# Layer one's sums over windows of 512 sorted edge rows in place of 1024, with three of each eight one-hots made on ScalarE

## The chip, the core and the metric

The kernel runs on one core of a Trainium2 chip. The core has five engines that run their own instruction streams and meet at semaphores: TensorE (PE in the profile, with its weight loads as PEld), VectorE (DVE), ScalarE (ACT), GpSimd (POOL) and SyncE (SP, here only an issuer of DMAs). The metric is the device time of one execution in microseconds, lower is better.

## What is computed

A graph network of 6250 nodes and 200000 edges, in two layers, each with a graph part, a mixing part and a feed-forward part. The change lies in the graph part of the first layer. For every edge there is a row of 128 numbers, and the rows have to be summed by source node:

```python
edge_proj = edge_attr @ W_sum + b_sum
sum3d = jax.ops.segment_sum(edge_proj, src, num_segments=num_nodes)
return x + z_in[in_deg] + z_out[out_deg] + cent_term + vor_term + sum3d
```

Since the projection is linear, the kernel sums the raw rows first and projects the 6250 sums afterwards.

## The kernel before

The nodes are cut into 50 tiles of P = 125. An earlier stage, which GpSimd's indirect DMAs bound, has written the edge rows to memory sorted by source tile (`rows_by_src`), 129 numbers a row: 128 values and the key, the source node. The stage under study starts when that is done, at 2187 us of the span, and ends at 2646 us.

It goes over **windows**: W1 consecutive sorted rows that belong to one tile. The number of windows is fixed when the program is built, NW1 = 248 for W1 = 1024, enough for any split of the edges over the tiles. A table on the core (`win1_s`, `win1_b`, `win1_base`) tells each window's first row, its tile and the tile's first node. For a window four engines do this:

- SP loads its rows into one of 8 slots of `win`, R1 = W1/128 = 8 rows on each of 128 partitions (L992). It reads eight windows' starts from the table at the top of a round, and for each load waits until PE has summed the window that had the slot.
- DVE makes the one-hot matrix (L1045): for each row and each of the 125 nodes of the tile, 1 where key minus base equals the node's number. That is one instruction over 128 x 1000, into one of 4 buffers of `hot`.
- PE multiplies (L1101): R1 matmuls of 128 x 128 values by 128 x 125 one-hot, added up in one of 4 PSUM banks. The float32 matmuls show as two passes each, so a window is 16 weight loads and 16 matmuls in the trace. PE waits for the one-hot, for the data, and until DVE has emptied the bank four windows back.
- DVE adds the bank to the tile's columns of `acc` (L1037), at a place that the table gives.

All four run in rounds of U = 8 windows, a hardware loop of 31 rounds whose first is written out. The order on DVE is fixed: one-hot of window s, then the addition of window s-2, for s = 0 to 7. Between one-hot 0 and the addition that follows it stands the load of eight tile numbers from the table into DVE's registers (`load_values`, L121). Each wait is a helper (`at`, L52 and L53): a wait, then an increment of a counting semaphore.

Beside it, until 2490 us, GpSimd gathers and adds the degree embeddings (`z_rows`), and DVE waits for it before the projection stage. ACT has nothing to do until the last window is added.

Of the kernel before, what the change touches and what calls it, by code (L numbers as in the profile page):

```python
# [18 lines left out]
ALU = mybir.AluOpType  # L19
ACT = mybir.ActivationFunctionType  # L20
# [3 lines left out]
P = 125  # L24
# [5 lines left out]
EPAD = EC - EF  # L30
TS = 256
PAD_KEY = 99999
W1 = 1024
R1 = W1 // 128
W2 = 256
NW1 = -(-((E + NT * (W1 - 1)) // W1) // 8) * 8
# [50 lines left out]
def program(nc, a, out):  # L87
# [875 lines left out]
    with s12, ExitStack() as ctx:  # L963
# [14 lines left out]
        accs_ready = sem("accs_ready")  # L978
        wsum_in, init2, hot_ready, win_summed, acc_done, y_ready, y_added = (
            sem(s) for s in ("wsum_in", "init2", "hot_ready", "win_summed", "acc_done", "y_ready", "y_added"))  # L980
        block = ctx.enter_context(nc.Block())

        @block.sync
# [42 lines left out]
        @block.vector  # L1026
        def _(dve):
            ch = chain("dve", dve)
            dve.wait_ge(init2, 1)

            def add(g, bank, b):
# [7 lines left out]
            def windows(i):  # L1039
                early = isinstance(i, int)  # L1040
                b = None
                for s in range(U):
                    at(dve, win_in[s], i * 16 + 16, passed["dve"])
                    keys = win[:, s * RC:(s + 1) * RC].rearrange("p (r c) -> p r c", r=R1)[:, :, ED]
                    dve.scalar_tensor_tensor(out=hot[:, (s % 4) * R1 * P:(s % 4 + 1) * R1 * P].rearrange("p (r n) -> p r n", r=R1),  # L1045
                                             in0=keys.unsqueeze(2).to_broadcast([128, R1, P]), scalar=win1_base[:, bass.ds(i * U + s, 1)],
                                             in1=iota_f[:, 0:P].unsqueeze(1).to_broadcast([128, R1, P]),
                                             op0=ALU.subtract, op1=ALU.is_equal).then_inc(hot_ready, 1)
                    if s == 0:
                        b = load_values(dve, win1_b, 0, U - 2, NT) if early else load_values(dve, win1_b, i * U - 2, U, NT)  # L1050
                    if not early:
                        add(i * U + s - 2, (s - 2) % 4, b[s])
                    elif s >= 2:
                        add(s - 2, (s - 2) % 4, b[s - 2])
# [24 lines left out]

        @block.scalar  # L1080
        def _(act):
            act.wait_ge(acc_done, NW1)

            def stage_acc(t, u, i):
# [7 lines left out]
        def _(pe):  # L1092
            def windows(i):
                for s in range(U):
                    g = i * U + s
                    at(pe, hot_ready, g + 1, passed["pe"])
                    at(pe, win_in[s], i * 16 + 16, passed["pe"])
                    if not isinstance(i, int) or s >= 4:
                        at(pe, acc_done, g - 3, passed["pe"])
# [1335 lines left out]
```

## Time and profile before

| | |
|---|---|
| median of 3 runs | 6528.96 us (6525.89 to 6530.78) |
| profiled execution, its own time | 6524.86 us |
| its span, first to last instruction | 6523.2 us |
| the stage under study | 2187 to 2646 us, 248 windows |
| PE, PEld, DVE, ACT busy over the span | 60%, 45%, 54%, 10% |

The span is what the chip's profiler saw of one execution, and the 1.7 us around it are start and end. Busy shares over the whole span say little here, since the stages have different limits. A row of a timeline is: start in us, length in us, engine, line, operation, what it writes and reads, and in brackets the idle time of the engine before it with what ended it. "issue" there means that the trace shows no wait. Engine names that end in q are the engine's instruction queue.

### The profile page before, as it was taken

The page shows a single profiled execution, that of the slowest core. Times are in us where ns is not written, and L with a number is a line of the kernel's source. Part 1 is how long each engine was busy: PE and PEld are TensorE (multiplying, and loading weights), DVE is VectorE, ACT ScalarE, POOL GpSimd, SP SyncE. Part 2 cuts the span into 40 slices and gives each one's busy share as a digit, 9 for nine tenths or more (in the row PEclk, how much of TensorE's full clock was granted, in tenths as well). Part 3 has the DMA queues.
Part 4 walks back from the last instruction along what each step waited for, and adds up shares of the span by engine and source line. Part 5 has one row for each costly group of instructions (what it writes and reads, how often), then busy time and mean ns, then how long its engine had stood idle before and what let it go on. Part 6 is the DMA issues. An engine that isn't in the chain of part 4 may idle for free. (4 is left out here: it accounts for less than half of the span.)

```text
span 6523.2 us, 84837 instructions
## 1 busy us (share of the span) xinstructions
PE 3916.1 (60%) x18036; PEld 2960.0 (45%) x18037; DVE 3514.9 (54%) x7152; ACT 677.8 (10%) x1606; POOL 3694.9 (57%) x3921
## 2 busy tenths in 40 slices
PE   0005666266640599899766676767677766317990
PEld 0004555154420599688544444444444444316770
DVE  9999999742223588824344444444444425731113
ACT  3000000212210000222100000000000002202320
POOL 1777777777777782000477777777777730051006
PEclk9999999999855799999777777777777768558995
DMA  3333333333333698100333333333333350111114
GB/s 94 103 103 102 99 100 102 100 101 98 102 102 102 235 333 301 59 1 6 105 103 104 103 104 103 103 104 103 103 103 103 104 57 2 61 68 64 63 61 125
DMA packets 382410, 666.59 MB, mean 102 GB/s; under 512 B 207743, under 2 KB 235991, under 8 KB 369671
## 3 DMA queue, kind: packets, MB, share of 16 engines
q0 software_dynamic: 148768, 375.57, 19.6%
q1 hardware_dynamic: 233575, 290.24, 15.3%
q8 instruction: 28, 0.46, 0.0%
q14 instruction: 39, 0.32, 0.0%
HBM read 519.29 MB, written 146.21 MB: 102 GB/s over the span
## 5 line engine op out<-in xcount | busy, mean ns | idle before, releaser
L1628 POOL DMA_INDIRECT rows<-projected_rows,pw_in x1664 | 1619.8, 973 | 989.4 <-issue 488.6
L576 POOL DMA_INDIRECT rows_by_src<-ring,stage x1563 | 1515.1, 969 | 484.6 <-issue 454.9
L1786 PE MATMUL pg<-rows,hot 128*125 128x256 f32 x3328 | 1279.4, 525 | 661.8 <-DMA rows<-projected_rows,pw_in 518.1
L1786 PEld LDWEIGHTS pg<-rows,hot 128*125 128x125 f32 x3328 | 764.7, 253 | 1160.9 <-issue 1057.9
L1644 DVE TENSOR_TENSOR agg<-agg,pg 125x256 f32 x832 | 349.1, 420 | 890.0 <-PE pg L1786 880.9
L1101 PE MATMUL pw<-hot,win 128*128 128x125 f32 x3968 | 453.1, 277 | 277.6 <-DVE hot L1045 274.9
L1101 PEld LDWEIGHTS pw<-hot,win 128*128 128x128 f32 x3968 | 448.3, 193 | 283.0 <-issue 282.4
L1693 DVE SCALAR_TENSOR_TENSOR hot<-pw_in,m_block_first,g_numbers 128x250 f32<-128x250 int32 x832 | 391.2, 470 | 296.7 <-issue 229.3
L808 PE MATMUL phist<-hi,lo 128*125 128x50 bf16 x3136 | 413.8, 281 | 219.3 <-DVE hi L608 219.3
L808 PEld LDWEIGHTS phist<-hi,lo 128*125 128x125 bf16 x3136 | 370.5, 222 | 264.0 <-issue 257.0
L1045 DVE SCALAR_TENSOR_TENSOR hot<-win,win_base,iota_f 128x1000 f32<-128x1000 f32 x248 | 340.5, 1373 | 137.2 <-POOL acc L1001 128.1
L2280 POOL DMA_DIRECT2D moe_results<-XT x56 | 34.1, 610 | 456.1 <-DVE XT L2296 456.1
L253 PE MATMUL pqkv<-d_cnt,lower 128*128 128x50 f32 x2 | 0.7, 434 | 439.0 <-DVEq L217 439.0
L2296 DVE TENSOR_TENSOR XT<-e_py,e_b 128x256 f32<-128x256 f32 x112 | 47.5, 424 | 368.4 <-PE e_py L2333 368.4
L2333 PE MATMUL e_py<-e_w,XT 128*128 x896 | 208.1, 385 | 45.1 <-ACT XT L2319 45.1
L605 DVE TENSOR_TENSOR lo<-pctx,lo_dst 128x1000 bf16<-128x1000 f32 x196 | 233.9, 1193 | 0.0
L605 DVE TENSOR_TENSOR lo<-pctx,lo_src 128x1000 bf16<-128x1000 f32 x196 | 231.2, 1179 | 0.0
L1732 ACT ACTIVATE m_kn<-m_kv 125x512 f32<-125x512 f32 x50 | 31.5, 630 | 1703.9 <-DVE m_kv L1662 1703.9
L627 DVE TENSOR_TENSOR_SCAN pqkv<-XT,first_src,pctx 128x448 f32<-128x448 bf16 (+2 forms) x200 | 205.8, 1029 | 0.0
L2352 PE MATMUL e_ph<-XT 128*128 128x256 f32 x896 | 204.5, 382 | 0.9 <-ACT XT L2314 0.9
L2333 PEld LDWEIGHTS e_py<-e_w,XT 128*128 128x128 f32 x896 | 165.7, 190 | 78.6 <-issue 58.4
L253 PEld LDWEIGHTS pqkv<-d_cnt,lower 128*128 128x128 f32 x2 | 0.5, 309 | 439.5 <-DVEq L217 439.5
(422 smaller groups left out, 5933.2 us busy)
## 6 DMA issues: line engine op xcount, KB each, us to landing
win<-rows_by_src SPq DMA_DIRECT2D x248, 516.0 KB, 5.0
ring<-in_edge_attr SPq DMA_DIRECT2D x97, 1024.0 KB
rows<-projected_rows,pw_in POOLq DMA_INDIRECT x1664, 2.8
rows_by_src<-ring,stage POOLq DMA_INDIRECT x1563
XT<-moe_rows SPq DMA_DIRECT2D x56, 256.0 KB
moe_results<-XT POOLq DMA_DIRECT2D x56, 256.0 KB, 2.3
pw_in<-pairs_by_dst SPq DMA_DIRECT2D x832, 2.0 KB
e_w<-in_L_ffn_W SPq DMA_DIRECT2D x16, 512.0 KB
```

What stands on the lines that cost most here:

```text
L576: pool.indirect_dma_start(rows_d, bass.IndirectOffsetOnAxis(ap=stage[:, h * HC + j:h * HC + j + 1].bitcast(U32), axis=0), ring4[:, h, j, : ...
L605: dve.tensor_tensor(lo1[:, u * 8 * P:(u + 1) * 8 * P].rearrange("p (c n) -> p c n", c=8), numbers[:, 0:P].unsqueeze(1).to_broadcast([Q, 8, ...
L627: dve.tensor_tensor_scan(pqkv[:, u, 0:n], masks[:, u, 0:n], pctx[:, 0, 0:n], first_src[:, bass.ds(b, 1)], ALU.add, ALU.bypass).then_inc(sc ...
L808: mm = pe.matmul(phist[0:P, 0, which * 64:which * 64 + NT], lo1[:, (u * 8 + j) * P:(u * 8 + j + 1) * P], hi1[:, (u * 8 + j) * NT:(u * 8 + ...
L1045: dve.scalar_tensor_tensor(out=hot[:, (s % 4) * R1 * P:(s % 4 + 1) * R1 * P].rearrange("p (r n) -> p r n", r=R1), in0=keys.unsqueeze(2).to ...
L1101: mm = pe.matmul(pw[:, s % 4, 0:P], win[:, s * RC + r * (ED + 1):s * RC + r * (ED + 1) + ED], hot[:, ((s % 4) * R1 + r) * P:((s % 4) * R1 ...
L1628: pool.indirect_dma_start(rows[:, (2 * (s % RU) + r) * D:(2 * (s % RU) + r + 1) * D], None, proj_d, bass.IndirectOffsetOnAxis(ap=pw_in[:, ...
L1644: dve.tensor_tensor(tile, tile, pg[0:P, bank, 0:D], ALU.add).then_inc(acc_done, 1)
L1693: dve.scalar_tensor_tensor(out=hot[:, (s % 4) * 2 * P:(s % 4 + 1) * 2 * P].rearrange("p (r n) -> p r n", r=2), in0=keys.unsqueeze(2).to_br ...
L1786: mm = pe.matmul(pg[0:P, s % 4, 0:D], hot[:, ((s % 4) * 2 + r) * P:((s % 4) * 2 + r + 1) * P], rows[:, (2 * (s % RU) + r) * D:(2 * (s % RU ...
L2333: mm = pe.matmul(py[:, v, 0:D], hT[:, (u * NH + m) * MW + v * 128:(u * NH + m) * MW + (v + 1) * 128], w2[:, bass.ds((e * NH + m) * D, D)], ...
L2352: mm = pe.matmul(ph[:, m, 0:MW], w1s[:, (2 * u + k) * EXP_H + m * 128:(2 * u + k) * EXP_H + (m + 1) * 128], xT[:, (2 * u + k) * MW:(2 * u ...
```

## The change

W1 goes from 1024 to 512, so R1 from 8 to 4, the one-hot from 128 x 1000 to 128 x 500, the matmuls of a window from 8 to 4, a load from 516 KB to 258 KB, and NW1 from 248 to 440. The rounds stay at eight windows, so there are 55 in place of 31. Windows 2, 5 and 7 of each round get their one-hot from ACT and not from DVE: first the distance base minus key for the window's four rows on each partition turned round (`rel`, Identity with a bias), then for each of the four rows the absolute value of rel minus the node's number (Abs, bias from `rel`), then 1 minus that, cut at zero (Relu). `minus_base`, the negated table of bases, is made once by DVE. The additions all stay on DVE.

```diff
--- before.py
+++ after.py
@@ -30,7 +30,7 @@
 EPAD = EC - EF
 TS = 256
 PAD_KEY = 99999
-W1 = 1024
+W1 = 512
 R1 = W1 // 128
 W2 = 256
 NW1 = -(-((E + NT * (W1 - 1)) // W1) // 8) * 8
@@ -978,6 +978,15 @@
         accs_ready = sem("accs_ready")
         wsum_in, init2, hot_ready, win_summed, acc_done, y_ready, y_added = (
             sem(s) for s in ("wsum_in", "init2", "hot_ready", "win_summed", "acc_done", "y_ready", "y_added"))
+        rel_ready, away_ready, act_hot_ready = (sem(s) for s in ("rel_ready", "away_ready", "act_hot_ready"))
+        rel = sbuf(ctx, "rel", [128, R1])
+        minus_base = sbuf(ctx, "minus_base", [128, NW1])
+        base_ready = sem("base_ready")
+        ACT_TURNS = (2, 5, 7)
+
+        def by_act(s):
+
+            return s in ACT_TURNS
         block = ctx.enter_context(nc.Block())
 
         @block.sync
@@ -1026,6 +1035,7 @@
         @block.vector
         def _(dve):
             ch = chain("dve", dve)
+            dve.tensor_scalar(minus_base[:], win1_base[:], -1.0, None, ALU.mult).then_inc(base_ready, 1)
             dve.wait_ge(init2, 1)
 
             def add(g, bank, b):
@@ -1040,12 +1050,14 @@
                 early = isinstance(i, int)
                 b = None
                 for s in range(U):
-                    at(dve, win_in[s], i * 16 + 16, passed["dve"])
+                    if not by_act(s):
+                        at(dve, win_in[s], i * 16 + 16, passed["dve"])
                     keys = win[:, s * RC:(s + 1) * RC].rearrange("p (r c) -> p r c", r=R1)[:, :, ED]
-                    dve.scalar_tensor_tensor(out=hot[:, (s % 4) * R1 * P:(s % 4 + 1) * R1 * P].rearrange("p (r n) -> p r n", r=R1),
-                                             in0=keys.unsqueeze(2).to_broadcast([128, R1, P]), scalar=win1_base[:, bass.ds(i * U + s, 1)],
-                                             in1=iota_f[:, 0:P].unsqueeze(1).to_broadcast([128, R1, P]),
-                                             op0=ALU.subtract, op1=ALU.is_equal).then_inc(hot_ready, 1)
+                    if not by_act(s):
+                        dve.scalar_tensor_tensor(out=hot[:, (s % 4) * R1 * P:(s % 4 + 1) * R1 * P].rearrange("p (r n) -> p r n", r=R1),
+                                                 in0=keys.unsqueeze(2).to_broadcast([128, R1, P]), scalar=win1_base[:, bass.ds(i * U + s, 1)],
+                                                 in1=iota_f[:, 0:P].unsqueeze(1).to_broadcast([128, R1, P]),
+                                                 op0=ALU.subtract, op1=ALU.is_equal).then_inc(hot_ready, 1)
                     if s == 0:
                         b = load_values(dve, win1_b, 0, U - 2, NT) if early else load_values(dve, win1_b, i * U - 2, U, NT)
                     if not early:
@@ -1079,6 +1091,27 @@
 
         @block.scalar
         def _(act):
+            def windows(i):
+                for k, s in enumerate(ACT_TURNS):
+                    n = i * len(ACT_TURNS) + k
+                    own = hot[:, s % 4 * R1 * P:(s % 4 + 1) * R1 * P]
+                    at(act, win_in[s], i * 16 + 16, passed["act"])
+                    if not isinstance(i, int) or k:
+                        at(act, away_ready, n * R1, passed["act"])
+                    keys = win[:, s * RC:(s + 1) * RC].rearrange("p (r c) -> p r c", r=R1)[:, :, ED]
+                    act.activation(rel[:], keys, ACT.Identity, bias=minus_base[:, bass.ds(i * U + s, 1)]).then_inc(rel_ready, 1)
+                    if not isinstance(i, int) or s >= 4:
+                        at(act, win_summed, i * U + s - 3, passed["act"])
+                    at(act, rel_ready, n + 1, passed["act"])
+                    for r in range(R1):
+                        act.activation(own[:, r * P:(r + 1) * P], iota_f[:, 0:P], ACT.Abs, bias=rel[:, r:r + 1], scale=-1.0).then_inc(away_ready, 1)
+                    at(act, away_ready, (n + 1) * R1, passed["act"])
+                    act.activation(own, own, ACT.Relu, bias=ones[:, 0:1], scale=-1.0).then_inc(act_hot_ready, 1)
+
+            act.wait_ge(base_ready, 1)
+            windows(0)
+            with act.Fori(1, NW1 // U) as i:
+                windows(i)
             act.wait_ge(acc_done, NW1)
 
             def stage_acc(t, u, i):
@@ -1093,7 +1126,11 @@
             def windows(i):
                 for s in range(U):
                     g = i * U + s
-                    at(pe, hot_ready, g + 1, passed["pe"])
+                    if by_act(s):
+                        at(pe, act_hot_ready, i * len(ACT_TURNS) + ACT_TURNS.index(s) + 1, passed["pe"])
+                    else:
+                        turn = s - sum(t < s for t in ACT_TURNS)
+                        at(pe, hot_ready, i * (U - len(ACT_TURNS)) + turn + 1, passed["pe"])
                     at(pe, win_in[s], i * 16 + 16, passed["pe"])
                     if not isinstance(i, int) or s >= 4:
                         at(pe, acc_done, g - 3, passed["pe"])
```

DVE's instructions from the top of its loop in the kernel before, where hot is a one-hot, win_b the table of tile numbers and acc<-acc,pw an addition; ISA and REGISTER_ALU rows are waits, increments and register arithmetic:

```order
L1057 ISA
L1045 ISA
L1045 SCALAR_TENSOR_TENSOR hot<-win,win_base,iota_f 128x1000
L121 ISA
L121 TENSOR_LOAD win_b
L52 REGISTER_ALU
L1037 ISA
L1037 TENSOR_TENSOR acc<-acc,pw 128x125
L1045 ISA
L1045 SCALAR_TENSOR_TENSOR hot<-win,win_base,iota_f 128x1000
```

The same place in the changed kernel, a few rows further:

```order
L1057 SCALAR_TENSOR_TENSOR hot<-win,win_base,iota_f 128x500
L121 ISA
L121 TENSOR_LOAD win_b
L52 REGISTER_ALU
L1047 ISA
L1047 TENSOR_TENSOR acc<-acc,pw 128x125
L1057 ISA
L1057 SCALAR_TENSOR_TENSOR hot<-win,win_base,iota_f 128x500
L1047 ISA
L1047 TENSOR_TENSOR acc<-acc,pw 128x125
L1047 ISA
L1047 TENSOR_TENSOR acc<-acc,pw 128x125
```

The load of the eight tile numbers stands where it stood, between the first one-hot and the first addition of a round, but a round is now half as many rows. Where a window has its one-hot from ACT, two additions follow each other.

ACT's instructions for the first window that it serves in a round (window 2), in the changed kernel; before, ACT had none in this loop:

```order
L1102 ACTIVATE rel<-win,minus_base 128x4
L52 REGISTER_ALU x2
L1107 ACTIVATE hot<-iota_f,rel 128x125 x4
L52 REGISTER_ALU
L1109 ACTIVATE hot<-hot,ones 128x500
```

Six instructions make one one-hot, and the second and third step each wait for the step before by a semaphore.

## Rows read from the trace of the kernel before

**Rows 1.** Windows view: stage under study in two parts, and two earlier stretches.

```profile
core 0: us, PE busy (x) PEld busy (x) DVE busy (x) ACT busy (x) POOL busy (x), PEclk, DMA share, GB/s
600.00:700.00 100.00, 64.29 (x505) 58.42 (x506) 100.00 (x127) 0.00 (x0) 76.60 (x89) 1.00 0.35 104
1800.00:1900.00 100.00, 62.03 (x122) 35.51 (x123) 13.24 (x31) 21.88 (x61) 75.63 (x88) 0.50 0.33 95
2187.00:2490.00 303.00, 298.22 (x2604) 295.15 (x2604) 265.98 (x327) 0.00 (x0) 263.76 (x201) 0.99 0.95 334
2490.00:2646.00 156.00, 154.92 (x1367) 153.13 (x1365) 123.97 (x170) 0.24 (x2) 0.00 (x0) 1.00 0.80 269
```

**Rows 2.** Groups by line, 2187 to 2646 us: busy us, mean ns, idle before.

```profile
L1101 PEld LDWEIGHTS pw<-hot,win 128*128 128x128 f32 x3968 | 448.3, 193 | 283.0 <-issue 282.4
L1045 DVE SCALAR_TENSOR_TENSOR hot<-win,win_base,iota_f 128x1000 f32<-128x1000 f32 x248 | 340.5, 1373 | 137.2 <-POOL acc L1001 128.1 <-issue 8.7 <-DMA win<-rows_by_src 0.4
L1037 DVE TENSOR_TENSOR acc<-acc,pw 128x125 f32 x248 | 69.6, 281 | 59.0 <-issue 33.4 <-PE pw L1101 24.4
```

**Rows 3.** Timeline of PEld, late in the stage.

```profile
2603.22 14.37 PEld L1101 LDWEIGHTS pw<-hot,win 128*128 128x128 f32 x128 [0.17 <-issue]
2617.77 14.37 PEld L1101 LDWEIGHTS pw<-hot,win 128*128 128x128 f32 x128 [0.18 <-issue]
2632.32 12.58 PEld L1101 LDWEIGHTS pw<-hot,win 128*128 128x128 f32 x112 [0.18 <-issue]
```

**Rows 4.** Timeline of DVE over the top of one round.

```profile
2612.77 0.28 DVE L1037 TENSOR_TENSOR acc<-acc,pw 128x125 f32 x1 [0.29 <-PE pw L1101]
2613.35 1.26 DVE L1045 SCALAR_TENSOR_TENSOR hot<-win,win_base,iota_f 128x1000 f32<-128x1000 f32 x1 [0.29 <-issue]
2615.76 0.28 DVE L1037 TENSOR_TENSOR acc<-acc,pw 128x125 f32 x1 [1.15 <-issue]
2616.00 1.26 DVE L1045 SCALAR_TENSOR_TENSOR hot<-win,win_base,iota_f 128x1000 f32<-128x1000 f32 x1
2617.18 0.28 DVE L1037 TENSOR_TENSOR acc<-acc,pw 128x125 f32 x1
```

**Rows 5.** Timeline of DVE, the same place while GpSimd adds.

```profile
2321.40 1.78 DVE L1045 SCALAR_TENSOR_TENSOR hot<-win,win_base,iota_f 128x1000 f32<-128x1000 f32 x1 [0.29 <-issue]
2323.80 0.28 DVE L1037 TENSOR_TENSOR acc<-acc,pw 128x125 f32 x1 [0.62 <-issue]
```

**Rows 6.** Line L121, register loads: count, ns min/median/max, when.

```profile
L121 DVEq TENSOR_LOAD <-win_b x1: 1861/1861/1861, 2613.5 to 2613.5; - x1
L121 DVEq TENSOR_LOAD <-win_b x1: 1852/1852/1852, 2321.5 to 2321.5; - x1
L121 SPq TENSOR_LOAD <-win_s x1: 525/525/525, 2616.9 to 2616.9; - x1
```

**Rows 7.** Line L53, PE's queue from 2616 to 2619 us.

```profile
L53 PEldq EVENT_SEMAPHORE  x5: 51/51/51, 2617.3 to 2618.8; - x5
```

**Rows 8.** The page's group of the second layer's one-hots.

```profile
L1693 DVE SCALAR_TENSOR_TENSOR hot<-pw_in,m_block_first,g_numbers 128x250 f32<-128x250 int32 x832 | 391.2, 470 | 296.7 <-issue 229.3
```

**Rows 9.** Groups of ACT by form, anywhere in the span.

```profile
L1458 ACT ACTIVATE f_hT<-f_ph,f_b 128x250 f32<-128x250 f32 x200 | 93.7, 469 | 210.0 <-PE f_ph L1493 210.0
L763 ACT ACTIVATE cv<-cv 125x512 f32<-125x512 f32 x50 | 31.5, 630 | 120.8 <-DVE cv L692 120.8
L1474 ACT COPY XT<-f_ptr 128x250 f32<-128x250 f32 x50 | 18.7, 374 | 2.2 <-PE f_ptr L1486 2.1
L1734 ACT ACTIVATE m_hv<-m_hv 125x16 f32<-125x16 f32 x50 | 10.8, 216 | 249.9 <-DVE m_hv L1666 225.8 <-issue 24.1
```

**Rows 10.** Timeline rows: two ACT instructions in a row; DVE after itself.

```profile
2712.21 0.83 ACT L1458 ACTIVATE f_hT<-f_ph,f_b 128x250 f32<-128x250 f32 x2
...
2041.39 0.43 DVE L752 TENSOR_TENSOR R<-R,mixed 125x256 f32 x1 [0.22 <-DVE mixed L751]
```

**Rows 11.** DMA issues, 2187 to 2646 us: KB each, us to landing.

```profile
win<-rows_by_src SPq DMA_DIRECT2D x242, 516.0 KB, 5.0
```

**Rows 12.** Line L240: one conversion of the window table.

```profile
L240 DVE CAST win_b<-ps_sort x2: 275/276/276, 70.0 to 70.7; 1x124 int32<-1x124 f32 x2
```

## The prediction, as it was put on record

> **What bounds the kernel now.** I read the windows view first. In the stage at issue, 2187 to 2646 us, PE's weight loads are busy 295 of 303 us and 153 of 156, at a granted clock of 0.99 and 1.00, while DVE is busy 266 and 124, and ACT not at all [rows 1]. So PE sets the pace, and the groups by line say how: 3968 loads for 248 windows [rows 2]. The timeline of PEld then shows what is not PE: 128 loads, one round of eight windows, take 14.37 us, and a new run of 128 starts every 14.55 us with 0.18 us idle ahead of it [rows 3]. Within a run the loads follow at (14.37 - 0.19)/127 = 0.1117 us, so a window's slot on PE is 16 x 0.1117 = 1.787 us and a round 14.30. The missing 0.25 us is a wait, one in each round.
>
> That wait is the key to the change, so I followed it. DVE's timeline over the top of a round [rows 4] gives all the links. PE's window 1 begins at 2603.22 [rows 3], so window 5 ends 5 x 1.787 later, at 2612.15, and its addition starts at 2612.77: **0.61** from the end of a slot to the addition, of which the last 0.29 is after PE's signal. Then one-hot 0 starts **0.58** later, the addition of window 6 **2.41** after it, one-hot 1 **0.24** after that. One-hot 1 ends at 2617.26, and PE's run starts at 2617.77: **0.51** from a one-hot that PE waits for to its first load. Added up from the end of slot 5 to the start of slot 1 of the next round: 0.61 + 0.58 + 2.41 + 0.24 + 1.26 + 0.51 = 5.61 us. PE has three windows to do in that time (6, 7 and 0), 3 x 1.787 = 5.36. The difference, 0.25, is the gap. So before, a chain of lags is just longer than the work that covers it.
>
> The 2.41 is a load of eight table values into DVE's registers, which takes 1.86 us; the addition behind it needs them [rows 6]. Where GpSimd's additions stretch the one-hot ahead of it to 1.78 us, the load takes 1.85 still and the addition comes 2.40 after the one-hot's start [rows 5, 6]. So it does not depend on how long the one-hot is.
>
> **The change, part by part.** *PE.* 440 windows of 8 passes are 3520 in place of 3968, a slot is 8 x 0.1117 = 0.893 us, a round 7.15. Alone that would be 440 x 0.893 = 393 us in place of 443.
>
> *DVE.* A one-hot over 128 x 500: the same operation takes 470 ns at 250 columns [rows 8] and 1.26 us at 1000 [rows 4], 1.05 ns a column, so 0.73 us. The mean over the stage is 1.373 for 1.26 [rows 2], because GpSimd's additions are in the way until 2490; for half the length and three fifths of the rounds I add 0.05. The additions, the load and the lags stay what they are.
>
> *The chain over a round*, walked as before, from the start of slot 1. Window 4 needs one-hot 4, which DVE does after addition 1: 0.89 + 0.61 + 0.24 + 0.73 + 0.51 = 2.98 to slot 4, while three slots are 2.68. Window 5 is ACT's. Its buffer is free when PE has done window 1: 0.89, and 0.48 until ACT starts (0.32 to PE's signal, as 0.61 less 0.29, and some 0.15 to react; between 0.32 and 0.61). ACT's costs come from [rows 9]: 630 ns at 512 columns and 216 at 16 give 0.203 us and 0.835 ns a column, and a bias read from memory 95 ns more (469 less 374, same shape). So Identity takes 0.30, an Abs 0.40, the Relu 0.72. Two in a row take 0.83, so the second starts 0.11 before the first ends [rows 10], and four Abs take 1.28. A step that waits for its own engine: 0.22, DVE's row [rows 10]; ACT shows none, and I bound it by 0.1 and by 0.37, the latter a third more than the 0.29 after PE's signal. Slot 5 then starts at 0.89 + 0.48 + 1.28 + 0.22 + 0.72 + 0.51 = 4.10 (Identity was done before) and ends at 4.99. From there to the next slot 1: 0.61 + 0.58 + 2.41 + 0.24 + 0.73 + 0.51 = 5.08. **A round takes 10.07 us**, 10.12 with GpSimd's 0.05. The gaps in it: 0.30 ahead of window 4 (2.98 - 2.68), 0.23 ahead of 5. Window 7 is ACT's again: its turn for window 5 ended at 3.59, the next takes 0.30 - 0.11 + 0.22 + 1.28 + 0.22 + 0.72 = 2.63, and with the 0.51 slot 7 starts at 6.73, 0.85 after slot 6 ends. Slots 7 and 0 end at 8.52, so ahead of window 1 PE waits 1.55, where it waited 0.25. A window took 14.6/8 = 1.83 us before and takes 1.27 now, for half the rows: the slots are halved and the lags are not.
>
> *PE's own queue.* Five semaphore increments, a window's three and two of the next, lie between 2617.3 and 2618.8 [rows 7], so the queue needs about 1.4 us for a window, 0.5 of it the waits and 0.9 the 16 passes. With 8 passes it is 0.95, just over the slot. It adds 0 to 0.05 a slot where slots follow closely; I take 0, since the chain above is not made of such slots.
>
> *Loads.* 440 of 258 KB in place of 248 of 516: 2.1 MB in 10.1 us, 209 GB/s where 334 and 269 were moved [rows 1]. They land in 5.0 us [rows 11], and a slot of `win` is free for over 5.5 us before ACT or DVE needs the next data in it, so they cost nothing; if they took over 6 they would come late for ACT first. SP's 8 x 0.33 us and its 0.5 us register load [rows 6] fit in a round.
>
> *Outside the loop.* The window tables are 440 wide in place of 248: about five operations of 96 columns more at 1.05 ns, on 275 ns each [rows 12], 0.5 us, ahead of the sort. `minus_base` lies under the 128 us that DVE waits for GpSimd [rows 2]; without that cover, 0.5 us.
>
> **Sum.** Before: 458.0 us (first one-hot at 2187.7 to the last addition's end) is 31 rounds of 14.6 and 5 of fill and drain. After: 55 x 10.12 = 556.6, and 2 for fill and drain of half-size windows: 558.6. The change is 100.6 + 0.5 = +101 us, on the profiled execution's own 6524.9: 6626. The median of before is 4 us above that execution, so I expect a median of **6628 us**.
>
> **A rule of the skill against the row.** The register load is the dearest link. The row says 1.86 us for eight values on DVE, and 0.53 us for eight on SP [rows 6]. The Trainium skill, DMA: Bandwidth & Descriptors, Latency and other measured facts, puts the floor of such a load at about 600 ns, and by that figure the sum would be 55 x 1.26 = 69 us less, 6559. DVE's own row does not agree with it, so it stays with 1.86.
>
> **The rivals.**
> 1. *The load follows the one-hot.* If the addition came 1.15 us after the one-hot's end [rows 4] and not 2.41 after its start, the link is 1.88 and a round 0.53 less: -29, 6599. Against it stands the stretched one-hot with 0.62 after it [rows 5]. 13%.
> 2. *The load gets cheap*, as on SP, 0.53: 55 x 1.33 = 73 less, 6555. Nothing in the change does it. 4%.
> 3. *ACT is slower.* If four Abs don't overlap (1.61) and its own wait is 0.37: +0.48 a round, +26, 6654. No such chain is in the trace. 12%.
> 4. *PE is the bound, as its weight loads say* (98% busy), and all lags hide: 393 us and 5 of ends, 398, -60: **6469, faster**. For it: DVE's one-hots, 340 us now [rows 2], come to 275 x 0.78 = 215. Against it: the gap that is there already [rows 3]. It decides from a round under (458 - 2)/55 = 8.3 us. The Trainium skill, Perfetto Trace Analysis, Identifying the Most-Contended Engine, takes LDWEIGHTS busy share as TensorE's measure and would have its work cut first, which is this outcome; the 98% agrees with it, the gap says that a chain stands right behind. 4%, and 1% for a round within 0.2% of no change.
> 5. *The clock falls.* PE's loads will be busy 393 of 559 us, 70%. At 64% busy the granted clock was 1.00 in one stretch, and at 62% it was 0.50, the 1.2 GHz level, in another [rows 1]. At half clock a slot is 1.79 us and a round at least 14.3: +230 for the whole stage, +58 for a quarter of it, 6686. Since the stretch at 64% kept the full clock over all its length and the new stage is above it, 4%.
>
> **Numbers.** My forecast holds 62%: 6628, from 6615 (the Relu and waits at their low bounds) to 6645. The range takes in rivals 1 and 3: 6585 to 6668, about 8 in 10. What a measurement tells from no change is some 0.2%, 13 us: faster 0.04, same 0.01, slower 0.95.
>
> **What would show it.** A PEld timeline with a gap of 1.3 to 1.6 us once in a round at window 1, smaller ones at 4, 5 and 7; rounds of 10.1 us; the addition behind the register load still 2.4 us after a one-hot of 0.73; ACT about 2.7 us a window and idle a fifth of the time; additions of windows 1 to 5 waiting for PE by 0.28, as before. The stage's end moves to about 2746 us, and nothing after it changes length. I am wrong if rounds are near 8 us, which would mean that DVE runs further ahead of PE than the order of its instructions lets me think, or if PEclk falls below 0.95 in the stage.

## The result and the profile after

| | before | changed |
|---|---|---|
| median | 6527.99 us of 4 runs (6525.89 to 6530.78) | 6642.22 us of 4 runs (6641.31 to 6644.89) |
| profiled execution, own time and span | 6524.86, 6523.2 us | 6642.16, 6640.5 us |
| first one-hot to the end of the last addition | 2187.7 to 2645.7, 458.0 us | 2192.8 to 2757.6, 564.8 us |

The ratio is 1.0175, 95% interval 1.0158 to 1.0193: slower, 14 us above the forecast of 6628 and inside its range. Of the +117.3 us between the two spans, 106.8 are the stage (forecast 100.6), 5.1 lie ahead of it (0.5) and 5.4 behind it (0).

The windows view of the changed kernel, which answers to [rows 1]:

```profile
core 0: us, PE busy (x) PEld busy (x) DVE busy (x) ACT busy (x) POOL busy (x), PEclk, DMA share, GB/s
2187.00:2430.00 243.00, 187.54 (x1440) 172.99 (x1440) 153.04 (x294) 151.41 (x407) 198.28 (x201) 0.97 0.83 256
2430.00:2700.00 270.00, 220.28 (x1715) 201.32 (x1714) 150.85 (x349) 180.44 (x483) 0.00 (x0) 1.00 0.74 211
```

No engine is the bound any more. PE's loads are busy 75% of the second stretch, where it was 98%, and DVE and ACT 56% and 67%. A round is 64 loads, so it takes 270 x 64/1714 = 10.08 us once GpSimd is done, which it is at 2419 us and not at 2484 as before.

PEld's timeline late in the stage, where [rows 3] showed one run of 128 loads a round:

```profile
2598.45 2.75 PEld L1138 LDWEIGHTS pw<-hot,win 128*128 128x128 f32 x24 [1.55 <-issue]
2601.48 2.88 PEld L1138 LDWEIGHTS pw<-hot,win 128*128 128x128 f32 x24 [0.28 <-issue]
2604.91 0.97 PEld L1138 LDWEIGHTS pw<-hot,win 128*128 128x128 f32 x8 [0.56 <-issue]
2606.05 0.97 PEld L1138 LDWEIGHTS pw<-hot,win 128*128 128x128 f32 x8 [0.17 <-issue]
2608.50 2.75 PEld L1138 LDWEIGHTS pw<-hot,win 128*128 128x128 f32 x24 [1.48 <-issue]
```

That is a round of 10.05 us: windows 1 to 3, then 4 to 6, 7, and 0. The gap of 1.48 us ahead of window 1 is the one that was 0.18. DVE's timeline over the same top of the round, to be read beside [rows 4]:

```profile
2604.01 0.28 DVE L1047 TENSOR_TENSOR acc<-acc,pw 128x125 f32 x1 [0.73 <-PE pw L1138]
2604.61 0.74 DVE L1057 SCALAR_TENSOR_TENSOR hot<-win,win_base,iota_f 128x500 f32<-128x500 f32 x1 [0.32 <-issue]
2607.01 0.28 DVE L1047 TENSOR_TENSOR acc<-acc,pw 128x125 f32 x1 [1.66 <-PE pw L1138]
2607.25 0.74 DVE L1057 SCALAR_TENSOR_TENSOR hot<-win,win_base,iota_f 128x500 f32<-128x500 f32 x1
```

The addition of window 5 starts at 2604.01, one-hot 0 0.60 later, and the next addition 2.40 after that. The view puts the 1.66 us ahead of it down to PE, but PE's window 6 was done before 2604.4. What was late is the load of the eight tile numbers, which starts beside one-hot 0 and outlasts it by 1.2 us, by the view of L121 in the same stretch:

```profile
L121 DVEq TENSOR_LOAD <-win_b x2: 1843/1846/1849, 2604.7 to 2614.8; - x2
```

One-hot 1 ends at 2607.99, and PE starts 0.51 after it. ACT's turn for windows 5 and 7:

```profile
2599.89 1.27 ACT L1107 ACTIVATE hot<-iota_f,rel 128x125 f32<-128x125 f32 x4 [2.46 <-PE pw L1138]
2601.28 0.71 ACT L1109 ACTIVATE hot<-hot,ones 128x500 f32<-128x500 f32 x1
2601.90 0.28 ACT L1102 ACTIVATE rel<-win,minus_base 128x4 f32<-128x4 f32 x1
2602.30 1.27 ACT L1107 ACTIVATE hot<-iota_f,rel 128x125 f32<-128x125 f32 x4
```

Its own waits are 0.12 (2601.28 less the end of the Abs at 2601.16), and the second turn starts 2.41 us after the first, where the forecast had 0.22 and 2.63.

PE's run 4 to 6 has a pause of 0.13 us inside it, which the view does not print, because a load lasts 0.19 us and the next one starts after 0.11. Asked from 2602.45 us on, it shows window 5's first load, 0.51 us after the end of ACT's Relu at 2601.99:

```profile
2602.50 0.97 PEld L1138 LDWEIGHTS pw<-hot,win 128*128 128x128 f32 x8
```

### The profile page after: what moved, and what is told of

It is laid out like the page before. It is cut to its first block and busy times, and to the rows that moved or that the text cites. A ratio compares the mean times of both kernels' runs of the same rounds, so it can differ in the third digit from the quotient of the medians.

```text
span 6640.5 us, 89830 instructions
## 1 busy us (share of the span) xinstructions
PE 3947.1 (59%) x17588; PEld 2949.7 (44%) x17589; DVE 3468.1 (52%) x7372; ACT 1048.2 (16%) x2596; POOL 3627.5 (55%) x3921
## 5 line engine op out<-in xcount | busy, mean ns | idle before, releaser
L1823 PE MATMUL pg<-rows,hot 128*125 128x256 f32 x3328 | 1326.6, 540 | 628.7 <-DMA rows<-projected_rows,pw_in 489.1
L1823 PEld LDWEIGHTS pg<-rows,hot 128*125 128x125 f32 x3328 | 790.8, 261 | 1141.6 <-issue 1031.2
L1138 PEld LDWEIGHTS pw<-hot,win 128*128 128x128 f32 x3520 | 417.5, 193 | 423.1 <-issue 416.8
L1047 DVE TENSOR_TENSOR acc<-acc,pw 128x125 f32 x440 | 124.6, 283 | 217.8 <-PE pw L1138 174.7
L1057 DVE SCALAR_TENSOR_TENSOR hot<-win,win_base,iota_f 128x500 f32<-128x500 f32 x275 | 223.8, 814 | 17.3 <-issue 17.3
L1107 ACT ACTIVATE hot<-iota_f,rel 128x125 f32<-128x125 f32 x660 | 209.2, 388 | 141.6 <-PE pw L1138 129.4
```

The costliest lines, as they stand in the source:

```text
L1107: act.activation(own[:, r * P:(r + 1) * P], iota_f[:, 0:P], ACT.Abs, bias=rel[:, r:r + 1], scale=-1.0).then_inc(away_ready, 1)
L1138: mm = pe.matmul(pw[:, s % 4, 0:P], win[:, s * RC + r * (ED + 1):s * RC + r * (ED + 1) + ED], hot[:, ((s % 4) * R1 + r) * P:((s % 4) * R1 ...
L1823: mm = pe.matmul(pg[0:P, s % 4, 0:D], hot[:, ((s % 4) * 2 + r) * P:((s % 4) * 2 + r + 1) * P], rows[:, (2 * (s % RU) + r) * D:(2 * (s % RU ...
```

## The experiments

All times are medians. The kernel before was measured beside each group of four kernels in the table: 6529.1 us beside the first four, 6533.0 beside the next four and 6539.7 beside the last four. It had 6528.0 beside the changed kernel, so an absolute time of a later group is not to be held against a forecast without taking 5 or 12 us off. The ratios are to the median beside each group; the stage is read from each trace as in the table above.

| kernel | median us | ratio to before (95%) | stage us |
|---|---|---|---|
| changed, fixed tiles | 6562.8 | 1.0052 (1.0036 to 1.0069) | 483.7 |
| changed, all one-hots on DVE | 6637.0 | 1.0166 (1.0149 to 1.0183) | 564.6 |
| changed, single loads | 6560.3 | 1.0045 (1.0028 to 1.0062) | 487.8 |
| changed, lag 3 | 6558.3 | 1.0050 (1.0033 to 1.0067) | 491.1 |
| changed, lag 3 and single loads | 6555.7 | 1.0034 (1.0021 to 1.0046) | 480.7 |
| before, lag 3 and single loads | 6522.8 | 0.9985 (0.9975 to 0.9994) | 447.8 |
| changed, wide, single loads | 6548.5 | 1.0024 (1.0014 to 1.0034) | 467.4 |
| changed, no GpSimd | 6636.1 | 1.0159 (1.0142 to 1.0176) | 555.6 |
| 768 rows, lag 3 and single loads | 6500.7 | 0.9939 (0.9926 to 0.9953) | 422.8 |
| 768 rows alone | 6568.2 | 1.0043 (1.0027 to 1.0058) | 489.6 |
| before, three one-hots on ACT | 6543.9 | 1.0007 (0.9998 to 1.0016) | 457.7 |
| changed, wide, one load | 6552.9 | 1.0021 (1.0011 to 1.0031) | 468.6 |

My theory throughout (A) is the prediction's: PE waits for a chain of lags over the top of the round, which did not shrink with the slots, and most of which is the register load.

**The two halves of the change apart.** All one-hots of the changed kernel on DVE:

```diff
-        ACT_TURNS = (2, 5, 7)
+        ACT_TURNS = ()
...
-            windows(0)
-            with act.Fori(1, NW1 // U) as i:
-                windows(i)
```

> The changed kernel with windows of 512 and every one-hot on DVE, none on ScalarE. Theory A: ScalarE's share hides nothing that matters, since each of its one-hots takes 2.6 us in which three slots of 0.89 pass, and DVE's chain over windows 1, 4 and 7 and over the register load is the same: a round of about 9.9 to 10.5 us, time 6640 to 6655 (about +7). Theory B: the chain of ScalarE goes away, a round falls to DVE's own work of 8.9 us, time about 6580. Theory D (the split is what keeps a bad change from being worse): a round of 11.5 or more, over 6700.

Measured 6637.0. And the kernel before, W1 = 1024, with windows 2, 5 and 7 on ACT (the edit is against the changed kernel):

```diff
-W1 = 512
+W1 = 1024
```

> The change without its smaller windows: W1 stays 1024, windows 2, 5 and 7 of each round have their one-hot from ScalarE. Theory A (the top of the round, one-hot 0, load, addition, one-hot 1, is DVE's in either case and sets the gap of 0.25 us; ScalarE's one-hot of 8 Abs and a Relu over 1000 columns, about 4.6 us, fits into four slots): rounds of 14.5 us as before, 6520 to 6535 us, no change. Rival J (the work given to ScalarE is itself a loss of some lag in each window it serves): 0.3 us or more in each of 31 rounds, 6540 or more. Rival K (DVE's time is what counts, and it is rid of 3 x 1.26 us a round): 6490 or less.

Measured 6543.9, ratio 1.0007 (0.9998 to 1.0016), no change that can be told. By its upper end alone rival J, 9 us more, would just fit, but the stage took 457.7 us for the 458.0 of before, and it would have been 9 longer. Its PEld timeline late in the stage is the one of before:

```profile
2604.50 14.37 PEld L1138 LDWEIGHTS pw<-hot,win 128*128 128x128 f32 x128 [0.20 <-issue]
```

So the loss is the window's, all of it; in these two comparisons ACT's one-hots are worth nothing either way. They take 3 x 1.26 us a round off DVE, which was not on the path except at the top of the round, and those instructions stayed. The kernel with all on DVE came out 3 us below the range that I expected (12 below its middle) and could have been better still. Late rounds without ACT took 9.8 us at the full clock, but the granted clock did not hold: in nine of the fifteen slices of 20 us from 2450 us on it was 0.91 or 0.92. Two of them:

```profile
2530.00:2550.00 20.00, 16.46 (x134) 15.24 (x133) 14.90 (x33) 0.00 (x0) 0.00 (x0) 1.00 0.76 220
2550.00:2570.00 20.00, 16.31 (x120) 15.36 (x120) 13.82 (x30) 0.00 (x0) 0.00 (x0) 0.91 0.68 197
```

133 loads at the full clock, 2.4 GHz, and 120 where part of the slice was granted 1.2 GHz. At the same clock ACT's one-hots thus made a round 0.25 us longer (10.05 for 9.8), which these slices gave back.

**The register load.** The changed kernel with additions at fixed tiles, so without the load (the sums are not those of the tiles):

```diff
                     if s == 0:
-                        b = load_values(dve, win1_b, 0, U - 2, NT) if early else load_values(dve, win1_b, i * U - 2, U, NT)
+                        b = [(v - 2) % U for v in range(U)] if not early else list(range(U))
```

> The changed kernel, but the additions go to fixed tiles of acc (0 to 7, by the window's place in the round), so DVE loads no tile numbers; the sums by tile are not what is computed then. Theory A (a chain of lags holds each round, and the register load of 1.9 us stands in it): the link from one-hot 0 to the next addition falls from 2.40 to about 0.7 us, the wait of PE at window 1 goes nearly away, a round goes from 10.04 to about 8.2 to 8.7 us, and the time falls by about 88 us to 6555. Theory B (ScalarE's one-hot chain holds the round): no change, 6640. Theory C (PE's instruction queue needs 1.25 us a window whatever DVE does): no change, 6640.

Measured 6562.8, with rounds of 8.5 us late in the stage: the load costs 79 us of the +114, where I expected 88. Then with the load kept, but one value at a time, each ahead of its own addition:

```diff
-                    if s == 0:
-                        b = load_values(dve, win1_b, 0, U - 2, NT) if early else load_values(dve, win1_b, i * U - 2, U, NT)
...
+                    if not early or s >= 2:
+                        b = load_values(dve, win1_b, i * U + s - 2, 1, NT)
+                        add(i * U + s - 2, (s - 2) % 4, b[0])
```

> The changed kernel, with each tile number loaded by itself just ahead of its addition in place of eight together at the top of the round. The second layer's expert stage has loads of one value at 0.30 us. Theory A: a load of 0.30 lies under the one-hot of 0.74 that DVE still works on, the link of 2.40 falls to about 0.85, and the wait moves to nothing: a round of 8.4 to 8.7 us, time about 6558. If instead what costs is the number of values and not that they stand together, eight times 0.3 come back elsewhere and a round stays at 10, 6642. Theory C: no change.

Measured 6560.3, as without any load. The view of L121 between 2600 and 2620 us:

```profile
L121 DVEq TENSOR_LOAD <-win_b x18: 299/301/318, 2601.4 to 2619.7; - x18
```

Eight values in one go take 1.85 us on this queue and one takes 0.30, so eight take 2.4 together; but spread over the round they lie under one-hots and waits. PEld's timeline shows windows 7, 0 to 3, 4 to 6 and 7 again: the gap at window 1 no longer shows, the largest is the one at window 7, and a round takes 8.6 us:

```profile
2601.45 0.97 PEld L1135 LDWEIGHTS pw<-hot,win 128*128 128x128 f32 x8 [0.53 <-issue]
2602.66 3.91 PEld L1135 LDWEIGHTS pw<-hot,win 128*128 128x128 f32 x32 [0.24 <-issue]
2606.73 2.87 PEld L1135 LDWEIGHTS pw<-hot,win 128*128 128x128 f32 x24 [0.16 <-issue]
2610.08 0.97 PEld L1135 LDWEIGHTS pw<-hot,win 128*128 128x128 f32 x8 [0.48 <-issue]
```

**The order of the additions.** If the chain's start is what matters (DVE's one-hot 0 stands behind the addition of window 5), then adding window s-3 in place of s-2 takes one slot off it:

```diff
-                        b = load_values(dve, win1_b, 0, U - 2, NT) if early else load_values(dve, win1_b, i * U - 2, U, NT)
+                        b = load_values(dve, win1_b, 0, U - 3, NT) if early else load_values(dve, win1_b, i * U - 3, U, NT)
...
-                        add(i * U + s - 2, (s - 2) % 4, b[s])
+                        add(i * U + s - 3, (s - 3) % 4, b[s])
...
```

> The changed kernel, with the addition of window s-3 in place of s-2 behind one-hot s: DVE runs one window further ahead of PE, with the same buffers and banks. Theory A: four slots of 0.89 now stand over the chain with the register load and three over the short chain of 2.1 us, so the round falls by most of two slots where it is the chain that holds it, to 8.7 to 9.0 us, time about 6570. Theory B and C: no change, 6640.

Measured 6558.3, 12 us better than expected: the load stayed and cost next to nothing. Either cure alone is worth 80 us or more, and after either the gap at window 1 no longer shows; if both act on that one gap, they do not add up. Both together:

> The changed kernel with both: the addition three windows behind, and each tile number loaded by itself. Theory A: no chain over the slots is longer than what covers it, and what is left is DVE's own work in a round, 4 x 0.66 + 8 x 0.24 and so on, 8.2 us, over PE's 7.15: stage about 454 us, time about 6537, hardly below the kernel before. Theory F (the two cures treat different waits and add up, each worth 82 us): 6475.

Measured 6555.7, hardly better than one, so the cures do not add up (rival F is out), but 19 us above what I expected (14 beside its own kernel before): a miss. The groups of that kernel from 2500 to 2600 us show who waits:

```profile
L1135 PEld LDWEIGHTS pw<-hot,win 128*128 128x128 f32 x753 | 87.2, 191 | 13.1 <-issue 11.9
L1104 ACT ACTIVATE hot<-iota_f,rel 128x125 f32<-128x125 f32 x142 | 45.0, 388 | 11.6 <-PE pw L1135 8.6
L1047 DVE TENSOR_TENSOR acc<-acc,pw 128x125 f32 x94 | 26.8, 285 | 25.7 <-PE pw L1135 20.3 <-issue 0.9
```

With four buffers and four banks ACT and DVE still wait for PE's slots, and PE for them. A second chain, from the end of a slot through ACT's one-hot to the slot four later (0.48 + 1.27 + 0.12 + 0.71 + 0.51 = 3.1 us against three slots, 2.7), had been hidden behind the first; it accounts for 0.4 a round, at window 5. The larger share I overlooked. ACT's turns for windows 5 and 7 follow each other at 2.41 us, and the two slots between them cover 1.79, so PE waits 0.62 at window 7. The timelines of ACT and then PEld in this kernel, where PE starts windows 5 and 7 each 0.51 us after the end of a Relu:

```profile
2560.02 0.71 ACT L1106 ACTIVATE hot<-hot,ones 128x500 f32<-128x500 f32 x1
2562.44 0.71 ACT L1106 ACTIVATE hot<-hot,ones 128x500 f32<-128x500 f32 x1
```

```profile
2561.24 1.86 PEld L1135 LDWEIGHTS pw<-hot,win 128*128 128x128 f32 x16 [0.32 <-issue]
2563.66 2.52 PEld L1135 LDWEIGHTS pw<-hot,win 128*128 128x128 f32 x20 [0.56 <-issue]
```

With the 0.08 by which a load outlasts the step to the next, these gaps are pauses of 0.40 and 0.64, and one of 0.25 ahead of window 0 is PE's own queue (below, at the walk over a round): 1.3 on 7.15 make 8.4, and 8.5 was measured. The pause at window 7 is there with 0.61 to 0.66 in all the kernels with windows of 512, ACT's turns and a lag of two or three windows. So I gave it 8 buffers and 8 banks, and let the additions lag by four, once with single loads and once with the one load of eight:

```diff
-        hot = sbuf(ctx, "hot", [128, 4 * R1 * P])
+        hot = sbuf(ctx, "hot", [128, U * R1 * P])
...
-        pw = psum(ctx, "pw", 4)
-        py = psum(ctx, "py", 2)
+        pw = psum(ctx, "pw", 8)
+        py = pw
```

> As the one above, but with eight one-hot buffers and eight PSUM banks (the projection's two banks shared with the sums') and the addition four windows behind. Theory A: buffers give nothing once DVE's own work is the bound, 8.0 to 8.2 us a round, time 6530 to 6537. If a wait for buffers was still in it (ScalarE's one-hots wait for the window four back), a round comes down to PE's 7.15 and the time to about 6480.

> The changed kernel with 8 one-hot buffers and 8 banks in place of 4, and the addition of window s-4, but with the one load of eight tile numbers a round (the wide kernel that ran before had eight single loads and took 8.45 us a round). Theory A (the load costs only where what waits behind it reaches PE; with four windows of lead 1.9 us are covered, and DVE is rid of eight single loads of 0.3 us with 0.5 us of waiting each where two additions follow each other): rounds of 7.7 to 8.1 us late in the stage, some 8.5 while GpSimd adds, the stage 440 to 455 us, 6505 to 6525 us. Rival L (something other than DVE's order holds the wide kernel, as the loads of rows or PE's queue): rounds stay at 8.4 or more, 6540 to 6555 us.

Measured 6548.5 and 6552.9: both misses in time. The first had the rounds of 8.1 that I expected late in the stage, but 8.7 beside GpSimd; the second had 8.2 and 8.7, with a time as rival L said and rounds shorter than it said. My account for the first (single loads that DVE can't hide where two additions follow each other) fell with the second kernel, where they are gone. The windows view and the groups of the second, 2500 to 2600 us, say what held it:

```profile
2500.00:2600.00 100.00, 95.17 (x781) 89.69 (x779) 67.49 (x157) 81.91 (x221) 0.00 (x0) 1.00 0.84 256
```

```profile
L1107 ACT ACTIVATE hot<-iota_f,rel 128x125 f32<-128x125 f32 x148 | 47.2, 391 | 4.6
L1109 ACT ACTIVATE hot<-hot,ones 128x500 f32<-128x500 f32 x37 | 26.4, 714 | 4.6
L1102 ACT ACTIVATE rel<-win,minus_base 128x4 f32<-128x4 f32 x36 | 10.6, 296 | 9.1 <-DMA win<-rows_by_src 8.4 <-issue 0.5
```

A round is 8.2 us (779 loads in 100), and ACT never waits for PE in it. ACT is busy 82 us of the 100, 9.7 more go into its own steps' lags and the issue, and 8.4 into rows that have not landed. `win` still has eight slots, so every window by which the one-hots run ahead of PE is taken from the time that its rows have to come. That ACT is the bound at three turns a round, with its data late, is what the rows point to; I did not try it with two turns or none, or with more slots, so it is not shown.

**GpSimd's share.** The changed kernel without the gathers and additions of the degree embeddings (they are missing from the output):

> The changed kernel without GpSimd's gathers and additions of the degree embeddings beside this stage; the embeddings are then missing from the output. Prices the contention that the forecast put at 0.05 us a round: rounds of 10.04 from the start, where they are 10.4 to 10.5 while GpSimd works, so 28 rounds x 0.4 = 11 us less, about 6631. If contention was nothing, 6642.

Measured 6636.1. Over the kernel before beside it that is 103.1 us, where the changed kernel was 114.2 over: 11 less, as expected. The stage is 555.6 us in place of 564.8, which is 55 rounds of 10.07 and 2. It also began 11.4 us later, and what follows it was 17.6 shorter; no run here says why, so I go by the stage. One slice of this kernel and then the same slice of the changed one:

```profile
2330.00:2350.00 20.00, 16.33 (x130) 14.92 (x129) 11.25 (x26) 13.46 (x36) 0.00 (x0) 1.00 0.74 212
```

```profile
2330.00:2350.00 20.00, 15.28 (x112) 14.30 (x112) 12.75 (x25) 12.17 (x33) 17.24 (x18) 0.91 0.81 235
2350.00:2370.00 20.00, 15.95 (x127) 14.86 (x128) 12.14 (x26) 12.76 (x36) 17.04 (x18) 1.00 0.87 273
```

Two things are lost beside GpSimd. At one place, behind the first 60 us, it is the clock, 0.91 over 20 us and 112 loads. Everywhere it is one-hots of up to 1.30 us in place of 0.74, where PE waits for them. From the changed kernel's timelines, a one-hot 4 and the run of PE that begins with window 4:

```profile
2302.80 1.24 DVE L1057 SCALAR_TENSOR_TENSOR hot<-win,win_base,iota_f 128x500 f32<-128x500 f32 x1
```

```profile
2304.55 2.75 PEld L1138 LDWEIGHTS pw<-hot,win 128*128 128x128 f32 x24 [0.74 <-issue]
```

0.51 after the one-hot's end again, and the gap is 0.74 where it is 0.28 late in the stage.

**The cure without the small windows.** The kernel before with lag 3 and single loads:

> The kernel before, windows of 1024 and all one-hots on DVE, with the addition three windows behind and single loads. Theory A: the wait of 0.25 us a round (0.4 while GpSimd works) goes, PE's loads follow without a gap, the stage goes from 458 to 31 x 14.30 + 5 = 448, time about 6518. Theory G (PE was the bound and these cures mean nothing at 1024): 6529.

Measured 6522.8, ratio 0.9985 (0.9975 to 0.9994), and a stage of 447.8 us for the 448 expected: the gap of 0.18 is gone, and PE's loads are busy all the time, by the windows view:

```profile
2500.00:2600.00 100.00, 100.00 (x898) 100.00 (x897) 85.24 (x112) 0.00 (x0) 39.94 (x26) 1.00 0.90 311
```

With that chain out of the way, fewer passes should pay. 768 rows a window, 312 windows, all one-hots on DVE:

```diff
-W1 = 1024
+W1 = 768
...
-        shift = width.bit_length() - 1
+        shift = 8 if width == W1 else width.bit_length() - 1
...
+        if width == W1:
+            ch.step(dve.tensor_scalar(col_i[0:NT, 0:1], col_i[0:NT, 1:2], 683.0, None, ALU.mult))
+            ch.step(dve.tensor_scalar(col_i[0:NT, 1:2], col_i[0:NT, 0:1], 11, None, ALU.arith_shift_right))
...
-                    if s == 0:
-                        b = load_values(dve, win1_b, 0, U - 2, NT) if early else load_values(dve, win1_b, i * U - 2, U, NT)
...
+                    if not early or s >= 3:
+                        b = load_values(dve, win1_b, i * U + s - 3, 1, NT)
+                        add(i * U + s - 3, (s - 3) % 4, b[0])
```

768 is no power of two, so the table of windows divides by it in two steps, a shift by 8 and then a product with 683/2048, about a third. The second kernel below keeps that part of the edit and leaves the additions and the one load as before.

> The kernel before with windows of 768 rows (312 of them, 12 passes each, 39 rounds), all one-hots on DVE, the addition of window s-3 in place of s-2, and each tile number loaded by itself ahead of its addition. Theory A (a round is the larger of PE's loads and the chain of lags; with one more window of lag and no eight-value load the chain is shorter than PE's 8 x 1.34 us): rounds of 10.7 to 11.1 us, the stage 39 x 10.7 to 11.1 and 5 of ends, 423 to 438 us in place of 458, so 6495 to 6510 us, faster than both kernels. Rival H (smaller windows lose by themselves, because each costs fixed time on DVE or in PE's queue): rounds over 11.5, the stage over 453, 6525 or more.

> The kernel before with windows of 768 rows alone: order of the additions and the one load of eight tile numbers as before, all one-hots on DVE. Theory A: the chain from the end of slot 5 to slot 1 is 0.61 + 0.58 + 2.41 + 0.24 + 1.00 + 0.51 = 5.35 us against three slots of 1.34, so a gap of 1.33 and rounds of 12.05, with GpSimd's stretching 12.2; the stage 475 to 481 us against 458, so 6546 to 6553 us. Rival H (what counts is the number of windows, in proportion): half way between 248 windows and the 440 of the changed kernel would be a third of +115, 6567. If the gap stays 0.25, 6500.

The first took 6500.7, ratio 0.9939: the fastest of all, and faster than the kernel before by 0.6%, of which 0.15 is what the two cures gave at 1024 rows. The stage, 422.8 us, lies at the low end of what I expected, with rounds of 10.7. PE's loads run through without a gap, even while GpSimd adds (busy 200.00 of 200 us from 2220 to 2420; the row is cut by the stretch asked for):

```profile
2299.84 46.31 PEld L1101 LDWEIGHTS pw<-hot,win 128*128 128x128 f32 x414
```

DVE is now close behind, busy 194 of 200 us between 2220 and 2420. The second, the smaller window alone, took 6568.2, ratio 1.0043: slower than before. Its rounds were 12.27 us late in the stage and not 12.05, from one run of loads to the next but one; the gaps are 0.33 and 1.07 for the 1.33 expected, and the loads fill 10.87 for 10.72. The stage was 489.6, not 475 to 481: 39 of the late rounds and 5 of ends make 482 or 483, and the other 7 lie beside GpSimd, where one-hots are stretched and a round takes 12.6. The median fell on the 6567 of rival H, by which the loss goes with the number of windows; but beside its own kernel before it is 28.5 us more, between the 18 to 25 of my account and the 39 of that rival. The time does not decide between them. The gap at window 1 does, since it grew from 0.18 to 1.07, and so does the first kernel, which has the same 312 windows and loses nothing. The same number of rows a window is thus 0.4% slower or 0.6% faster, by the lag of the additions and the way the tile numbers are loaded.

```profile
2606.74 1.42 PEld L1104 LDWEIGHTS pw<-hot,win 128*128 128x128 f32 x12 [0.33 <-issue]
2609.22 9.45 PEld L1104 LDWEIGHTS pw<-hot,win 128*128 128x128 f32 x84 [1.07 <-issue]
```

## Why the prediction was right

- *The chain over the top of the round.* Right in every link: 0.61, 0.60 for 0.58, 2.40 for 2.41, 0.24, 0.74 for 0.73, 0.51. Taking the load out or spreading it, or starting the chain a window earlier, each gave 79 to 84 us back.
- *The walk over a round.* 10.05 us measured where GpSimd is done, 10.07 forecast, but so close only by luck, since two errors cancel. Counted from load to load (the gaps of the view and 0.08 more), the pauses were 1.56 for the 1.55 forecast (window 1), 0.36 for 0.30 (4), 0.13 for 0.23 (5), 0.64 for 0.85 (7), and 0.25 ahead of window 0, where the forecast had none. The pauses at 5 and 7 are 0.31 shorter, since ACT's waits for itself are 0.12 and not 0.22.
- *PE's own queue, taken at 0*, is the term that was mis-sized against it: 0.25 us a round, some 14 us in the stage, all at the end of PE's loop body. Its branch and the three waits of window 0 stand in the queue behind window 7:

```profile
L1143 PEldq COMPARE_BRANCH  x1: 208/208/208, 2605.1 to 2605.1; - x1
L53 PEldq EVENT_SEMAPHORE  x3: 51/51/51, 2605.5 to 2606.0; - x3
```

  Window 0 starts at 2606.05, 0.70 us after one-hot 0 has ended at 2605.35, where it would start 0.51 after it if it waited for that alone. Every kernel with windows of 512 and ACT's turns has a pause of 0.22 to 0.27 there, with and without GpSimd and for each order of the additions; no run takes the branch away, so this is read from rows and not shown by an experiment.
- *GpSimd's 0.05 a round, 3 us in all*, was mis-sized: 9.2 us by the stages, 11 by the medians. Where PE has no slack left, a one-hot that is stretched by 0.5 us just ahead of a window that PE waits for is paid in full. I had scaled the mean over the stage instead of asking which one-hots are on the path. The round went from 10.07 to 10.5 us over 22 rounds. This includes the clock's dips, which I can't part from it.
- *Loads cost nothing.* Right: 3.1 us to land, and the changed kernel's ACT waited for rows 1.9 us in 100, where it had time to spare.
- *Outside the loop, 0.5 us.* The second half of the tile table is converted at 72.3 us for 70.7, so 1.6:

```profile
L240 DVE CAST win_b<-ps_sort x2: 374/374/374, 71.5 to 72.3; 1x220 int32<-1x220 f32 x2
```

  I had counted the wider operations and not PE's share between them. The other 3.5 us ahead of the stage, and the 5.4 behind it, lie where I found no instruction that the change touches. The stage's first one-hot stood at 2191.3 to 2204.2 us in the traces of the other kernels with smaller windows, but also at 2193.7 in one with 1024 rows, and the time behind the stage in that with all on DVE was 3877.3, as before. So executions differ by as much; no run settles what sets it.
- *The signs named ahead.* The gap at window 1, the rounds and the 2.4 us behind the one-hot came as said. ACT took 2.41 us a window and not 2.7, and was idle a third of the time; the additions waited 0.61 to 0.73 us for PE and not 0.28; the stage ended at 2757.6 and not 2746. None of these was on the path that sets the round except ACT's.
- *Rivals 1 and 2* (a cheaper load) don't hold: the addition came 2.40 us after the start of a one-hot of 0.74, and the load took 1.85. The floor of about 600 ns that the Trainium skill gives for such a load (DMA: Bandwidth & Descriptors, Latency and other measured facts) fits neither row here: 1.85 us for eight values is three times that, and 0.30 for one lies below it. *Rival 3*: four Abs overlap, 1.27, and ACT's own wait was shorter and not longer. *Rival 4*: a round took 10.05 us and not under 8.3; PE's busy share was no measure of the bound once its work fell. *Rival 5*: the clock did dip, but for few slices: 0.97 as a mean to 2430 us and 1.00 after.

Slower by 0.2% and more was right. The sum itself makes 6630 (6626 and the 4 us by which the median lay above the profiled execution), where 6628 was written. Between the profiled executions 16 us are missing: 6.2 in the stage, where GpSimd's term was 6.4 too small, 1.1 for the tables, and 8.9 ahead of the stage and behind it, which is as much as executions of other kernels differ there. The changed kernel's median lies on its profiled execution and not 4 above, which takes 4 of these back.

## What to carry to other kernels

Before a tile is made smaller, walk the loop once from an engine's slot back to itself and write down which links scale with the tile; where fixed lags are already just longer than the work that covers them, halving the tile only lengthens the gap. Take the fixed links off the path first (a longer lag between stages, scalars loaded one by one next to their use), and only then cut the padding: the same smaller window went from +0.4% to -0.6% by that. Count too how far apart an engine's turns lie against the slots between them, and what the end of the loop costs on each queue. An engine that waits in such a loop is not helped by taking work off it, as the three one-hots given to ScalarE show.

## What the hardware showed that I had not expected

- Eight scalars loaded at once into VectorE's registers take 1.85 us in the loop; the instruction ahead of the load goes on beside it, what stands behind waits. One value takes 0.30, on the same queue. Eight on SyncE take 0.52.
- GpSimd's two additions for a tile took 985 and 1568 ns as medians beside the kernel before, and 737 and 730 beside the changed one, so that its work ended 65 us earlier. From 2220 to 2420 us the mean of its instructions was 1.29 us beside the kernel before, 1.16 and 1.17 beside the two with one-hots of 750 columns, and 0.96 to 1.02 beside one-hots of 500, with 0.96 and 0.97 whether VectorE was busy 62% there (the changed kernel) or 82% (all one-hots on it). The length of VectorE's instructions alone does not set it, though: beside one-hots of 1000 columns it was also 1.05, with three of eight of them on ScalarE and VectorE busy 60%, and 1.57, with lag 3 and single loads and VectorE busy 86%, less than the 89% of the kernel before. What does is open.
- The granted clock was 1.00 through all of the stage but its start where PE's loads were 98% busy. It fell to 0.91 or 0.92 in single slices of 20 us where they were 70 to 80% busy: one in the changed kernel (and 0.94 and 0.98 in the two slices after its first), nine in that with all one-hots on VectorE, all of them after GpSimd was done, and none after the first two in that without GpSimd's work, where the loads were 75% busy. No row here says why it fell in one and not in the other.
